# A graph layer on one core: pair products of normalized keys read one operand from PSUM

## The reference

```
qn = _normalize(q) * (scale * temperature)
kn = _normalize(k) * scale
vN = v1 / N                                   # v1 = (1, v)
kv_mod = einsum('bhni,bhnj,bhne->bhije', kn, kn, vN)
kv = einsum('bhnd,bhne->bhde', kn, vN)
y = A * einsum('bhni,bhnj,bhije->bhne', qn, qn, kv_mod) + scale**2 * Bc * einsum('bhnd,bhde->bhne', qn, kv) + ...
```

## Time and profile before

| | us |
|---|---|
| runs before: median (lowest to highest) | 1453.89 (1453.29 to 1457.96) |
| the profiled execution, device time | 1454.93 |
| its span, first to last instruction | 1452.8 |
| steps 8 to 28, pair products and two batches a step | about 324 to 571 |
| steps 29 to 32 | about 571 to 604 |
| last part of the mix branch, 57 steps | about 604 to 926 |

### The profile page before, as it was taken

One profiled execution on the slowest core, in us unless ns is written; L12 is line 12 of the kernel. 1 busy time (PEld: TensorE's weight loads), 2 busy tenths in 40 slices (PEclk: granted clock), 3 DMA queues, 4 the chain that ended last, 5 costly groups with the idle time before them and its releaser, 6 DMA issues.

```text
span 1452.8 us, 25219 instructions
## 1 busy us (share of the span) xinstructions
PE 1210.4 (83%) x7992; PEld 869.7 (60%) x7993; DVE 848.5 (58%) x1771; ACT 601.5 (41%) x1947; POOL 735.3 (51%) x626
## 2 busy tenths in 40 slices
PE   3789956758777877799999999365899999999994
PEld 2545533425444544455554556265799999999994
DVE  8598859788888887554545455697323222332221
ACT  1300011443444345487777777251333333333331
POOL 2070000788888888777777777550233333333331
PEclk9999966878899888999999999756999999999998
DMA  5635374422222223343343344583122222222223
GB/s 180 207 130 187 139 281 139 141 78 77 77 77 74 80 77 87 98 117 109 113 116 114 103 115 113 222 343 142 30 38 37 36 36 36 36 36 36 36 36 103
DMA packets 67569, 153.67 MB, mean 106 GB/s; under 512 B 12961, under 2 KB 41558, under 8 KB 66262
## 3 DMA queue, kind: packets, MB, share of 16 engines
q0 software_dynamic: 32640, 75.27, 21.0%
q1 hardware_dynamic: 33478, 74.93, 14.6%
q10 hardware_dynamic: 1360, 2.33, 0.5%
HBM read 131.76 MB, written 23.92 MB: 107 GB/s over the span
## 4 chain that ended last, share of the span: by engine, by line
PE 61%; DVE 21%; POOL 7%; issue 5%; DMA 4%; ACT 1%; DVEq 1%; SPq 0%; POOLq 0%; ACTq 0%
PE ps L1543 14%; PE ps L1553 13%; PE ps L1250 13%; POOL arena L847 6%; DVE arena L1809 6%; PE ps L1191 4%; PE ps L1446 3%; PE ps L1458 2%; PE ps L1279 2%; PE ps L1200 1%; PE ps L1158 1%; DMA h_d<-arena 1%; DVE arena L1769 1%; DVE arena L1777 1%; PE ps L1404 1%
## 5 line engine op out<-in xcount | busy, mean ns | idle before, releaser
L847 POOL DMA_INDIRECT arena<-h_d,tables x440 | 516.0, 1173 | 134.0 <-issue 131.3
L1250 PE MATMUL ps<-arena 128*128 128x264 f32 x880 | 251.3, 441 | 89.6 <-DVE acc L1818 61.6
L1250 PEld LDWEIGHTS ps<-arena 128*128 128x128 f32 x880 | 184.6, 218 | 149.0 <-issue 97.2
L964 ACT ACTIVATE arena<-arena 128x64 f32<-128x64 f32 x880 | 222.0, 338 | 37.1 <-DMA arena<-h_d,tables 37.1
L889 POOL DMA_INDIRECT sum_d<-acc,tables x56 | 89.7, 1601 | 253.4 <-DVE acc L2197 245.8
L1543 PE MATMUL ps<-acc 128*128 128x128 f32 x1792 | 210.2, 276 | 0.0
L1543 PEld LDWEIGHTS ps<-acc 128*128 128x128 f32 x1792 | 205.6, 193 | 0.1
L1553 PE MATMUL ps<-arena,acc 128*128 x896 | 202.5, 379 | 0.0
L1553 PEld LDWEIGHTS ps<-arena,acc 128*128 128x128 f32 x896 | 166.0, 190 | 20.3
L1120 ACT ACTIVATE acc<-ps,b_s 128x128 f32<-128x128 f32 x448 | 128.1, 369 | 119.0 <-PE ps L1543 119.0
L2185 DVE COPY acc<-arena 128x1024 f32 x112 | 78.2, 699 | 121.7 <-PE ps L1543 120.8
(11 more groups left out here) (366 smaller groups left out, 1532.7 us busy)
## 6 DMA issues: line engine op xcount, KB each, us to landing
arena<-dl_d SPq DMA_DIRECT2D x22, 640.0 KB, 7.2
arena<-lo_d SPq DMA_DIRECT2D x16, 784.0 KB, 4.6
arena<-h_d,tables POOLq DMA_INDIRECT x440
arena<-in_w SPq DMA_DIRECT2D x4, 1664.0 KB, 12.3
arena<-in_w SPq DMA_DIRECT2D x4, 1632.0 KB, 25.2
arena<-hi_d SPq DMA_DIRECT2D x16, 343.0 KB, 5.1
h_d<-arena SPq DMA_DIRECT2D x25, 128.0 KB, 2.0
sum_d<-res SPq DMA_DIRECT2D x5, 640.0 KB, 8.6
```

The costliest lines, as they stand in the source:

```text
L847: pool.indirect_dma_start(gb[u][:, k, 0:D], None, h_d, bass.IndirectOffsetOnAxis(tsrc[:, j:j + 1], 0)).then_inc(s_gg[u], 16)
L964: ins = A_.activation(v, v, ACT.Copy, scale=wm[:, m + k, h:h + 1])
L1250: last = MM(ps[:, 6 + s, 0:ACOL], oh[b % OB][:, m, :], gb[u][:, m, :], start=(k == 0), stop=(k == TE - 1))
```

## The change

For tiles 5 to 24, ScalarE copies the 48 columns (k and its wrapped columns) of all 8 heads, 384 elements a partition, from `ext` to PSUM bank 5 (`windows`, once a tile, between `squares(t)` and `q_out(t - 2)` in the step that makes them). The copy waits for the wrapped columns (its own engine's) and for both pair products of the tile before, or, the first time, for the last reading of bank 5 by `local_values`. VectorE's pair product then takes k1 from bank 5 and k0 from `ext` as before, and waits in addition for the copy. Sizes, order and the rest of the work stay.

```
+        T_KP = 5
+        KW = MD + SQ
+        kwin = ps[:, 5, 0:MH * KW].rearrange("p (h c) -> p h c", c=KW)
+        assert T_KP + 2 >= S_LOC + 1
...
+            def windows(t):
+
+                act.wait_ge(s_kx, t + 1)
+                if t == T_KP:
+                    act.wait_ge(s_dv, NL // 2)
+                else:
+                    act.wait_ge(s_phi, KD * t)
+                A_.copy(kwin, ext[t % XE][:, :, MD + 1:EW]).then_inc(s_kp, 1)
...
                 if t < NT:
                     squares(t)
+                if T_KP <= t - 2 < NT:
+                    windows(t - 2)
                 if 0 <= t - 2 < NT:
                     q_out(t - 2)
...
-                o = g * QC * EW + MD + 1
-                k0 = ap(e_, o, [list(e_.ap[0]), [EW, QC], [0, SQ - 1], [1, MD]])
-                k1 = ap(e_, o + 1, [list(e_.ap[0]), [EW, QC], [1, SQ - 1], [1, MD]])
+                w, o, n = e_, g * QC * EW + MD + 1, EW
+                k0 = ap(w, o, [list(w.ap[0]), [n, QC], [0, SQ - 1], [1, MD]])
+                if t >= T_KP:
+                    dve.wait_ge(s_kp, t - T_KP + 1)
+                    w, o, n = kwin, g * QC * KW, KW
+                k1 = ap(w, o + 1, [list(w.ap[0]), [n, QC], [1, SQ - 1], [1, MD]])
                 V.tensor_tensor(phi[g]..., k0, k1, ALU.mult).then_inc(s_phi, 1)
```

More of the change, by code:

```diff
@@ L443, in gps_layer @@
         s_phi = sem("pair_features")
+        s_kp = sem("k_windows_in_psum")
         s_kv = sem("pair_features_used")
```

## The result

The changed kernel takes 1447.21 us, the median of 7 runs (1443.35 to 1450.44), against 1453.89 of before (7 runs, 1448.21 to 1457.96). The ratio is 0.995, with a 95% interval from 0.9931 to 0.9968, that is 4.7 to 10.0 us less. The profiled execution after the change is the shortest of its seven, 1443.35 us (span 1441.3), and that of before was above its median, so the two traces stand 11.5 us apart, where the medians stand 6.7 apart.

The account below looks back on a forecast made before the run. It took TensorE as the bound from 604 to 882, VectorE's chain in pair steps, and late POOL gathers at the seams; 2.4, 1.3 and 2.8 make 6.5 us off 1453.89, giving 1447.4, rounded to 1447.5; range 1442 to 1455.

Parts of the forecast that it names:

- What frees POOL: Pair stage: the PSUM operand removes the hold on gathers by 40 of 50 pair products, 2.7 us a step.
- Rival (2): Pair stage: the operand in PSUM does not free POOL, so the time stays at 1454 us; chance 0.06.
- The copy, the wait, the operand: Tiles 5 to 24: a 0.5 us copy in ScalarE's idle time, satisfied waits and PSUM reads all cost nothing.
- Rival (3): Pair products: long overlapping PSUM reads slow VectorE's chain, net +4.1 to +6.1 us, 1458 to 1460; chance 0.13.
- The lead at 571: End of pair stage: POOL is nearly 8 batches ahead of TensorE instead of 5.
- Term (a): At 602.97: TensorE's 2.38 us idle, for scaling that waited for a gather's landing, all goes: 2.4 us.
- rival (5): Steps 29 to 32 and narrow last steps: earlier landings shrink waits there too, 3 to 6 us more, 1443; chance 0.11.
- From 604 to 882: TensorE is the bound and gives nothing back; POOL's ring fills again by 882, a lead of 6 to 8.
- 15 us of head start: POOL's gain by 571: 3 batches at 5 us each, to remove TensorE's waits around 600, 910 and 921.
- (b): At 910.13: TensorE's 1.28 us idle for L2010, late because L1833 waited for a landing, goes: 1.3 us.
- (c): At 921.87: TensorE's 2.83 us idle for the last batch, whose scaling waited for a landing, goes: 2.8 us.
- rival (4): Pair stage: TensorE's clock can turn one or two steps either way, 1.6 us each; included in the forecast's 0.48.

Follow-up runs that it names:

- e1: Changed kernel with copy and wait kept, but both operands of all pair products read from SBUF: 1451.53 us, ratio 0.9994 to before.
- e5: The changed kernel itself, measured again on a second chip: 1447.86 us, ratio 0.9943 to before.
- e2: Changed kernel with the copy and PSUM operand only for the last ten tiles, 15 to 24: 1448.57 us, ratio 0.9968 to before.
- e3: Changed kernel with the copy and PSUM operand only for tiles 5 to 14: 1448.62 us, ratio 0.9971 to before.
- e7: Changed kernel with the last aggregated batch's two sums moved ahead of the step's first pair product: 1432.15 us, ratio 0.9853 to before.
- e9: e7 with the first batch's preparation ahead of the second pair product and its two sums right behind it: 1423.26 us, ratio 0.9799 to before.
- e6: Changed kernel with the copy and PSUM operand only for the last five tiles: 1446.57 us, ratio 0.9943 to before.
- e4: Changed kernel with POOL allowed only 5 batches ahead of TensorE instead of 8: 1457.00 us, ratio 1.0032 to before.

## Why the prediction was right, point by point

The time was right (1447.5 forecast, 1447.21 measured), inside the forecast's own range; two of its three terms were not what they were said to be.

- **What frees POOL.** Right. The hold goes with the PSUM operand and stays without it (0.972 and 1.378 us, e1). The rule of the Trainium skill that the instruction of two SBUF inputs contends with GpSimd (SBUF — State Buffer, Who interferes with whom) is borne out for indirect gathers, which read their row numbers from SBUF: 44 of 44 are held in before. Its inference that `tensor_tensor` leaves descriptor generation alone does not carry over to them; for transfers that read nothing in SBUF no run here tests it. Rival (2) falls.
- **The copy, the wait, the operand.** Right. The copy takes 0.468 us, between the bounds; e1 puts its cost at zero within 0.9994 (up to +0.6 us at the interval's upper end). L1829 takes 2.150 with the PSUM operand, 2.154 before. Rival (3), with 13 in 100 the largest threat, falls. L1829 shows nothing of the 65 ns more for a PSUM source that stood beside the sum by the Trainium skill (VectorE: DVE Perf Modes, errata section): by that it would be 2.22 us, an estimate.
- **The lead at 571.** Nearly right: 7.0 batches at batch 39 (the forecast said nearly 8, from 5), and POOL waits 61.3 us over 19 steps, 3.2 each, where 2 to 3 was said.
- **Term (a), 2.4 us: mis-sized.** Batches 45 to 54 gave 5.4 us, in after and again in e5, against the one trace of before (3.1 against e1's). In e5, e2 and e3 the six batches ahead of them give 1.4 back, where the granted clock lies at 0.50 once more (in e5 from 586.3 to 589.6), so over 39 to 54 the seam is worth 4.0 to 5.4. The failed step is the sentence that VectorE's and ScalarE's waits for landings after 604 lie beside TensorE's work. The one of 3.64 us at 606.62 does not: it makes TensorE idle 1.62 at 608.73, and with the 2.38 that makes 4.0. With the 0.26 at 623.71 and smaller pieces the idle times come to 4.4; the last 1.0 us is no idle time in the rows, and where it lies is open. That was rival (5), which I gave 0.11.
- **From 604 to 882.** TensorE is the bound, as said: 256.5 us from batch 54 to 102 in every kernel (256.9 in e1). But the ring does not fill again: the lead is 3.0 at batch 54 and 4.0 at 102, not 6 to 8. Of after, from 604 to 882, POOL's gathers (busy, count, PEclk, DMA, GB/s), then TensorE's edge matmuls (PE, PEld, the same three):

```profile
604.00:882.00 278.00, 213.43 (x213) 1.00 0.39 113
...
604.00:882.00 278.00, 102.80 (x418) 77.07 (x418) 1.00 0.39 113
```

  POOL issues 213 / 4 = 53.2 batches, TensorE sums 418 / 8 = 52.2: it gains one. The forecast had spent the same 15 us of head start twice. At the first seam TensorE moves forward and eats it: the lead there falls from 7.0 to 3.0, against 5.0 to 2.25 before.
- **Terms (b) and (c), 4.1 us.** The trace of after has 3.9 less at the end, and for the wrong reason. (b) is gone, 1.3 us, but it is gone in e1 too, which has both operands in SBUF. (c) is not: TensorE idles 2.11 for the last batch instead of 2.83, and what else is won there is that the matmuls behind it take 2.02 and not 2.71, with the clock. In e5 the wait is 3.77, the matmuls 3.86, and the end as long as before's. The wait is gone and the end 29 us only where the lead at batch 102 is above 4: 5.0 in e7 and e9, and 4.25 in e2, the one trace of a kernel with the old order of sums that wins all of (c):

```profile
907.75 4.16 PE L1267 MATMUL ps<-arena 128*128 128x264 f32 x16 [0.44 <-DVE acc L1838]
```

  These sixteen matmuls are the last two batches, one directly behind the other.
- **The clock.** Foreseen as rival (4), and seen in its size: where the step keeps 13.4 us in most cases, as said, before has one shorter step of 11.8, after three of 11.9. Eighteen steps take 238.6 and 234.8 us in these two traces, but 236.9 in e5, 236.3 and 236.2 in e2 and e3, and 238.6 and 238.8 in e1 and e6. The short step of before and the one after it (PE, PEld, DVE, ACT, POOL busy, PEclk, DMA, GB/s):

```profile
427.00:438.80 11.80, 9.09 (x78) 5.42 (x74) 11.02 (x20) 5.99 (x25) 9.67 (x8) 1.00 0.26 75
438.80:452.20 13.40, 10.69 (x78) 6.74 (x74) 11.21 (x20) 5.99 (x25) 10.96 (x9) 0.87 0.30 83
```

  In the short one the granted clock stays at 1.00, and TensorE's 78 matmuls take 1.6 us less; the short steps of after are of the same kind. The 3.8 us between the traces are most of the 5.0 us that the traces show until batch 39, and I don't count it for the change: the seam's 5.4 leave 1.3 of the medians' 6.7 for all else, with an interval from -0.7 to 4.6. Whether a pair stage without held gathers has such short steps more often is open: among these 18 there are three in after, two in e5, and one each in before, e1, e4 and e6.

So 6.5 came true as 4.0 to 5.4 at the first seam and 1 to 3 us for all else, where the forecast had 2.4 and 4.1. Two errors of opposite sign nearly cancelled: that the total was met to 0.3 us is luck. How often the end is won stays open, since only profiled executions tell it, and there are two of the changed kernel and one of before.

## What to carry to other kernels

Here an engine that only issues transfers was worth nothing by its busy time and something by its lead: count how many buffers it is ahead where the stage ends, and price a batch of lead by the seam behind it, once and not twice (here 4.2 us a batch up to a lead of 6, and at that seam nothing above). If gathers are longer than their free duration, look for the instruction with two SBUF operands that they start under, and move one operand to PSUM by an engine that idles. And when a step is longer than its busiest engine's work, look for the small instruction that both engines wait for in turn: moving two accumulates of 0.42 us brought 15 us, and the next move 9.

## What the runs showed of the hardware

- A gather that POOL starts while VectorE works on an instruction with both tensor operands in SBUF ends as if it began 0.12 to 0.13 us before that instruction's end (44 of 44 under the pair products of before); under the pair product with one operand in PSUM it takes its free 0.95. The means of the pair stage are 0.972 against 1.378 to 1.427.
- PSUM as one of the two sources costs VectorE nothing at this length: 2.150 against 2.154 us for 1920 elements, with windows that overlap.
- ScalarE writes 384 elements from SBUF to PSUM in 0.468 us.
- An idle time of 2.11 us left TensorE's granted clock at 1.00, one of 3.77 saw it at 0.50 and cost the eight matmuls behind it 1.84 us.
